# Token attention: the score products of one batch mixed with the query and key projections of a batch two periods younger

## The reference

```python
def _L1_attn_b_ref(x, Wq, Wk, Wv, Wo, bo, lq1, lq2, lk1, lk2):
    q = _split_qk(x @ Wq.T, b, n) * SCALE      # (b, n, 32 half-heads, 8)
    k = _split_qk(x @ Wk.T, b, n)
    v = (x @ Wv.T).reshape(b, n, H, 2 * D).transpose(0, 2, 1, 3)
    att = jax.nn.softmax(jnp.nan_to_num(jnp.einsum('bnqd,bnkd->bnqk', q, k)), axis=-1)
    diff = att[:, :, :H, :H] - lam * att[:, :, H:, H:]
    out = jnp.einsum('bnah,bhnd->bnad', diff, v)
    out = out * rsqrt(mean(out * out, -1) + EPS) * (1.0 - LAM_INIT)
    return out.reshape(b, n, DIM) @ Wo.T + bo
```

## Time and profile before

| | |
|---|---|
| median of three runs | 1204.39 us (1202.14 to 1208.55) |
| the profiled execution: its span | 1204.3 us |
| busy in it: PE, DVE, ACT, GpSimd | 1006.6, 714.8, 367.6, 319.5 us |
| span of B1's scores, first of batch 0 to last of batch 7 | 799.5 to 1034.8 us |

### The profile page before, as it was taken

The page is one execution under the profiler, slowest core; times in us unless marked ns, Lnnn a source line. Parts: engine busy times, 40 slices in busy tenths (PEclk is TensorE's granted clock), DMA queues, the critical chain, the costliest instruction groups (busy, mean ns, idle before and its releaser), DMA issues.

```text
span 1204.3 us, 21333 instructions
## 1 busy us (share of the span) xinstructions
PE 1006.6 (84%) x8146; PEld 883.3 (73%) x8146; DVE 714.8 (59%) x1323; ACT 367.6 (31%) x663; POOL 319.5 (27%) x352
## 2 busy tenths in 40 slices
PE   3589988665779787788879999998888887799998
PEld 3466755445667665656658999998888887799998
DVE  4458775534667777876664554545566654644443
ACT  2136554422322222242333322321222221232222
POOL 4102220027754573221110031100333332330000
PEclk9569998886889989987768999976677775599999
DMA  8735340000120002554410000335666665210000
GB/s 231 213 117 169 125 117 24 2 1 18 28 79 1 1 1 65 172 175 124 134 33 1 2 1 1 74 78 105 122 132 131 132 132 88 36 36 10 19 18 19
DMA packets 147429, 89.38 MB, mean 74 GB/s; under 512 B 109632, under 2 KB 136256, under 8 KB 146560
## 3 DMA queue, kind: packets, MB, share of 16 engines
q1 hardware_dynamic: 142960, 70.45, 24.0%
q10 hardware_dynamic: 2944, 12.59, 3.6%
q0 software_dynamic: 1424, 4.98, 1.4%
HBM read 54.16 MB, written 33.55 MB: 73 GB/s over the span
## 4 chain that ended last, share of the span: by engine, by line
PE 63%; DVE 19%; issue 6%; ACT 4%; SPq 3%; DMA 2%; POOL 2%; DVEq 0%; ACTq 0%; POOLq 0%
PE SC L373 16%; PE SC L2145 9%; PE pb L373 8%; PE OT L373 7%; PE pa L373 4%; PE OT L1893 3%; DVE mx L1319 3%; PE SC L1846 2%; PE SC L1875 2%; PE OT L2172 2%; PE OT L2070 2%; PE pa L2340 2%; DMA b_Q<-q_groups 1%; DVE OS L1487 1%; DVE ON L1676 1%
## 5 line engine op out<-in xcount | busy, mean ns | idle before, releaser
L373 PE MATMUL SC<-xT_h,w_h 128*128 128x256 f32 x512 | 148.6, 290 | 10.0 <-DVE xT_l L1736 7.8
L373 PE MATMUL SC<-xT_l,w_h 128*128 128x256 f32 x512 | 146.9, 287 | 0.0
L373 PE MATMUL SC<-xT_h,w_l 128*128 128x256 f32 x512 | 146.1, 285 | 0.0
L373 PEld LDWEIGHTS SC<-xT_h,w_h 128*128 128x128 f32 x512 | 98.9, 193 | 13.4 <-DVE xT_l L1736 11.5
L1319 DVE TENSOR_REDUCE mx<-SC 128x4 f32<-128x1024 f32 x64 | 78.1, 1221 | 48.3 <-PE SC L1846 47.9
L373 PE MATMUL OT<-w,Qs 128*128 128x256 f32 x768 | 104.3, 285 | 2.2 <-DVE Qs L1746 1.4
L373 PEld LDWEIGHTS SC<-xT_h,w_l 128*128 128x128 f32 x512 | 99.1, 194 | 0.0
L373 PEld LDWEIGHTS SC<-xT_l,w_h 128*128 128x128 f32 x512 | 98.6, 193 | 0.0
L373 PEld LDWEIGHTS OT<-w,Qs 128*128 128x128 f32 x768 | 96.4, 191 | 2.8 <-DVE Qs L1746 1.6
L1742 DVE TENSOR_TENSOR hidden_f<-SC,silu_gate 128x512 f32<-128x512 f32 x64 | 44.1, 689 | 76.7 <-ACT silu_gate L1199 76.7
L1746 DVE TENSOR_TENSOR Qs<-hidden_f,Qs 128x512 fp32r<-128x512 f32 x64 | 44.7, 698 | 44.7 <-ACT Qs L1207 44.7
(11 more groups left out here) (413 smaller groups left out, 2693.7 us busy)
## 6 DMA issues: line engine op xcount, KB each, us to landing
Qs<-q_stack SPq DMA_DIRECT2D x56, 128.0 KB, 2.9
k_stack<-KT_h SPq DMA_DIRECT2D x16, 256.0 KB, 2.4
k_stack<-KT_l SPq DMA_DIRECT2D x16, 256.0 KB, 3.0
q_stack<-QT_h SPq DMA_DIRECT2D x16, 256.0 KB, 2.2
q_stack<-QT_l SPq DMA_DIRECT2D x16, 256.0 KB, 2.8
b_Q<-q_groups SPq DMA_DIRECT2D x64, 64.0 KB
o_groups<-b_O ACTq DMA_DIRECT2D x8, 512.0 KB, 2.9
Qs<-q_stack SPq DMA_DIRECT2D x56, 64.0 KB, 3.1
```

What stands on the lines that cost most here:

```text
L373: ins = pe.matmul(out_ap, left[a], right[b], start=first and n == 0, stop=last and n == len(terms) - 1, **more)
```

## The change

The work on each batch stays the same; its place changes. `q_out` and `k_out` no longer issue their products: they only hold their waits. The new `mixed(g, h)` issues the 32 score products of half h of batch b and, between them, the 12 projection products of batch b+2: those of the queries in half 0, those of the keys in half 1. One projection product follows each second or third score product, and the twelfth follows the last. What leads up to the projections and what follows them is moved to fit:

- x_turned(b+3), and the high and low parts of x, come one slot earlier, in slot 7, and so before y_out and turned of the next period
- the parts of Q are made in slot 0 (two slots earlier), those of K in slot 1 (two slots earlier)
- stats, rstd and xn come one slot earlier (3, 4 and 6).

v_out, the stores and the loads keep their slots. In DVE's `at_slot` the line of less_maximum(b, 0) stands ahead of that of K's low part, and both are due in slot 1; weights_of(b, 0) is due in slot 2. On ACT, load_k and load_q of batch b+1 stand ahead of K's high part in slot 1.

```diff
--- before.py
+++ after.py
@@ -809,7 +809,7 @@
                             prepare([A0_JOBS[g]])
 
                 def tokens_at(g):
-                    for b in due(g, -19):
+                    for b in due(g, -20):
                         rstd_of(b)
                     for b in due(g, 11):
                         clipped(b)
@@ -1140,13 +1140,13 @@
                         load_k(b)
                     for b in due(g, -7):
                         load_q(b)
-                    for b in due(g, -16):
+                    for b in due(g, -17):
                         high(b, x_pair(s, b), pa, "xT", "vp", 1, "xh")
                     for b in due(g, 18):
                         high(b, aT, OT[1], "aT", "y", 1, "ah")
-                    for b in due(g, -14):
+                    for b in due(g, -16):
                         high(b, QT, pb, "qp", "qstore", 64, "qh")
-                    for b in due(g, -13):
+                    for b in due(g, -15):
                         high(b, KT, pa, "kp", "kstore", 64, "kh")
                     for b in due(g, 3):
                         probs(b, 1)
@@ -1607,17 +1607,17 @@
                         less_maximum(b, 1)
                     for b in due(g, 18):
                         low(b, aT, OT[1], "ah", "al")
-                    for b in due(g, -14):
+                    for b in due(g, -16):
                         low(b, QT, pb, "qh", "ql")
                     for b in due(g, 13):
                         square_sums(b)
-                    for b in due(g, -13):
+                    for b in due(g, -15):
                         low(b, KT, pa, "kh", "kl")
                     for b in due(g, 4):
                         weights_of(b, 1)
-                    for b in due(g, -20):
+                    for b in due(g, -21):
                         stats(b)
-                    for b in due(g, -17):
+                    for b in due(g, -18):
                         normalise(b)
                 return at_slot
 
@@ -2122,11 +2122,19 @@
                     wait("xres", b - 5, 1)
                     if b == 0:
                         split_done(pe, "attn_b1")
-                    channels_out(pb, wq, "qp", x_pair(s, b))
 
                 def k_out(b):
                     wait("xl", b, 1)
-                    channels_out(pa, wk, "kp", x_pair(s, b))
+
+                def projected(b, ps, w, signal, n):
+
+                    of = x_pair(s, b)
+                    o, t, term = n // 6, n % 6 // 3, n % 3
+                    i, j = ((0, 0), (0, 1), (1, 0))[term]
+                    ins = pe.matmul(ps[:, o * S:(o + 1) * S], w[i][:, t, o * P:(o + 1) * P], of[j][:, t, :],
+                                    start=t == 0 and term == 0, stop=t == 1 and term == 2)
+                    if n == 11:
+                        ins.then_inc(sig.sem[signal], 1)
 
                 def v_out(b):
                     wait("ql", b, 1)
@@ -2139,11 +2147,28 @@
                     wait("clamped", b - 1, h + 1)
                     if b == 0:
                         item(pe, F5, "g_hid", B - 1, 3 + h)
+
+                def scored(b, h, n):
+
                     Kg = b1_K[b % 2].rearrange("p (k g) -> p k g", g=GROUPS)
+                    g = HALVES * h + n
+                    ins = pe.matmul(SC[h][:, 32 * n:32 * n + 32], b1_rows(Qg, g), b1_rows(Kg, g), start=True, stop=True)
+                    if n == HALVES - 1:
+                        ins.then_inc(sig.sem["scores"], 1)
+
+                def mixed(g, h):
+
+                    front, back = due(g, h - 16), due(g, h)
+                    for b in front:
+                        (q_out, k_out)[h](b)
+                    for b in back:
+                        scores(b, h)
                     for n in range(HALVES):
-                        g = HALVES * h + n
-                        ins = pe.matmul(SC[h][:, 32 * n:32 * n + 32], b1_rows(Qg, g), b1_rows(Kg, g), start=True, stop=True)
-                    ins.then_inc(sig.sem["scores"], 1)
+                        for b in back:
+                            scored(b, h, n)
+                        for b in front:
+                            if n * 12 // HALVES < (n + 1) * 12 // HALVES:
+                                projected(b, (pb, pa)[h], (wq, wk)[h], ("qp", "kp")[h], n * 12 // HALVES)
 
                 def b1_rows(q, g):
                     return q[0:96, :, g]
@@ -2191,20 +2216,15 @@
                     for h in range(TT):
                         for b in due(g, 8):
                             turned(b, h)
-                    for b in due(g, -16):
+                    for b in due(g, -17):
                         x_turned(b)
                     for h in range(TT):
                         for b in due(g, 9):
                             attend(b, h)
                     for h in range(TT):
-                        for b in due(g, h):
-                            scores(b, h)
+                        mixed(g, h)
                     for b in due(g, 18):
                         a_turned(b)
-                    for b in due(g, -14):
-                        q_out(b)
-                    for b in due(g, -13):
-                        k_out(b)
                     for b in due(g, -12):
                         v_out(b)
                 return at_slot
```

## The result

The changed kernel takes 1280.9 us (median of 4, 1276.0 to 1287.6), the kernel before 1203.3 us (median of 4). The ratio is 1.0655, with a 95% interval of 1.0616 to 1.0695: slower by 78 us. The forecast was 1281. Some executions of a kernel fall in a slower state of the chip, and the ratios here, and the medians of kernels 2 and 8, are of the others alone, so that they can differ by a tenth of a per cent from the quotient of two medians.

What follows compares the result with a forecast made beforehand. PE was taken as fullest but not quite full, its 13.8 us gap ending in a wait for DVE's xn. Stall and dearer halves summed to +56 us (full clock) or +83.9 (half); +77 taken on 1204 gave 1281, range 1248 to 1308.

Steps and rivals of the forecast that it cites:

- The stall on DVE: K's low part waits past the second half's scores, pushing weights_of(b, 0) and later work back: steady gap +11.3 us at half clock.
- T: The end of the second half's score products of batch b, from which the gap to the next batch is counted.
- ACT's load issues: K's high part on ACT stands behind load_q's four DMA issues, which add 2.9 us to DVE's wait.
- y_out and turned: PE work at the gap's end, after x_turned: 2.72 and 3.51 us at half clock.
- The halves: 32 score products with 12 wide ones between: 9.28 us at half clock or 8.39 at full, against 6.94 for narrow alone.
- Rival 2: Switching does not overlap: each wide product costs load plus stream, 0.40 us; about 1300 us and up; 7 in 100.
- wide products wholly hidden: Lower bound of a mixed half: wide products vanish under narrow loads, leaving 6.94 us.
- rival 1: Same stall, cheap halves: clock stays full or wide products hide beneath narrow loads; 1260 down to 1243 us; 14 in 100.
- Three quarters of the way to half clock: Clock assumed between the sums at full clock (+56 us) and half clock (+83.9): +77 us.
- mixing by itself is near nothing: Two halves cost +4.8 us per period against 3.76 leaving the gap; net within -3.8 to +6.
- the landing at +13: The b_Q loads land about 13 us after the second half's scores, taken as hidden in the longer gap.
- Rival 3: Wide products vanish under narrow loads and DVE is not late: six gaps lose 3.76 us each, 1182 us; 4 in 100.

Runs made afterwards that it cites:

- Kernel 2: The changed kernel with only ACT's K high part moved ahead of load_q, behind load_k: 1263.0 us, 1.0507 of before.
- kernel 8: The kernel before, unmixed, with the younger batch's norm made earlier from batch 3 on: 1199.2 us, 0.9961 of before.
- Kernel 1: The changed kernel with only DVE's K low part moved from slot 1 to slot 2: 1238.2 us, 1.030 of before.
- kernel 7: The kernel before with one more wait: DVE begins weights_of(b, 0) only after both halves of batch b's scores: 1223.0 us, 1.0158 of before.
- kernel 4: The changed kernel with both moves, K low in slot 2 on DVE and K high ahead of load_q on ACT: 1234.0 us, 1.0274 of before.
- kernel 5: kernel 4 with the younger batch's statistics, root, xn and x_turned made earlier from batch 3 on: 1224.9 us, 1.0205 of before.
- kernel 10: kernel 5 with the b_Q loads split six on SP and six on ACT: 1226.8 us, 1.021 of before.
- kernel 9: kernel 8 with the b_Q loads split six on SP and six on ACT: 1199.2 us, 0.9978 of before.
- Kernel 6: kernel 5 unmixed, each half's 32 score products first and its 12 projection products behind them: 1218.2 us, 1.0142 of before.
- kernel 3: The changed kernel, same slots, unmixed: each half's 32 score products first, then its 12 projection products: 1270.8 us, 1.0572 of before.

## Why the prediction was right

**The stall on DVE** was right in place and size. Expected after T: KT_l done at 4.2, weights_of(b, 0) 7.55, less_maximum 11.3, weights_of(b, 1) 16.4, xn 17.85, x_turned 18.9. Read: 4.2, 7.6, 11.3, 16.1, 17.5, 18.6. Kernel 1 shows the cause, by an edit on DVE alone that takes 43 us away; kernel 7 shows a part of it, by a wait that brings some 20 us into the kernel before.

**ACT's load issues** as a part of the stall: right. Kernel 2 gives 18 us for a wait that is 2.4 to 2.6 us shorter in six periods, where 17 was expected (12.5 us of it stand in the gaps of its trace), and kernel 4 shows that the issues cost only in the stall's shadow.

**y_out and turned** were priced at half clock throughout, 6.2 us, and then a quarter of the way back: they took 2.56 and 1.9, that is 4.5, behind batch 3. The granted clock was 0.50 in y_out, 0.85 in the first microsecond of turned and 1.00 in the second. The gap was 23.1, where the sum at half clock had 25.1. Batches 0, 1 and 5 measured 21.4, 21.4 and 19.1 against 21.1, 21.7 and 19.3.

**The halves** were expected at 9.28 us at half clock and 8.39 at full. They took 8.8 to 9.2, and 0.2 for the last wide product. The mixed stretch can be read in the chain of batch 3, at both clocks:

```profile
932.17 0.22 PE pb L2134
932.39 0.55 PE SC L2155 x3
...
938.11 0.40 PE pb L2134
938.50 0.45 PE SC L2155 x3
```

One wide and three narrow products take 0.77 us at full clock and 0.85 at half. Three narrow alone are 0.65, so a wide one adds 0.12 or 0.20: the 0.121 and 0.195 of the forecast, which came from a wide run's pace and from one switch. By the Trainium skill ("TensorE: Matmul & The Clock Gate", section LDWEIGHTS) a load of 128 columns takes an estimated 107 ns, and a wide product would have added that at half clock. The trace does not agree: it has 0.20. Rival 2 (0.40 each) and wide products wholly hidden are both excluded, and so is the cheap end of rival 1.

**The match to a microsecond is luck.** Three quarters of the way to half clock was a choice between +56 and +83.9. The trace has 75.2, which is 69% of the way, and the four executions lie 12 us apart. Batches 2 to 4 lost 14.2, 13.7 and 13.7 us, where the sum has 16.1 at half clock and 10.65 at full. Two small things stood at nothing: batch 6 gained 1.6 us, and the first score product came 1.4 us later.

**What was wrong** is a sentence that did not enter the sum: that mixing by itself is near nothing, since 3.76 us leave the gap. They do not come off the gap. Once the stall is taken away (kernels 5 and 10), the gaps of batches 0 to 5 are 12.2 to 14.6 us, where they were 13.3 to 14.2 before. The chains behind batch 4 end in the wait for b_Q, which is there 13.1 to 13.9 us after its first issue, whoever issues it, and the wide products had lain beside that transfer. The prediction had read the landing at +13 and called it hidden, but did not set it against the 3.76. So the mixed halves cost their full 2.1 us each, 12 halves or 25 us, and kernel 5 is 24 us behind the kernel before. Rival 3 with its 1182 us was out of reach for the same reason: in the steady batches the transfer holds the gap at about 13 us.

The loss by its parts, from the differences of the ratios (6.55, 3.00, 2.74 and 2.05%, of 1203 us): 43 us by the keys' low part ahead of weights_of(b, 0), 3 more with ACT's order (within the noise of the two runs), 8 by the norm and x_turned in the tail (kernel 4 to 5), and 25 by projections moved from beside the b_Q transfer into the halves. Each difference is uncertain by several microseconds. The last part is borne out by kernels 9 and 10: they differ by the projections' place and the queue moves that go with it, and 24.5 us of the difference of their traces lie in the halves. Kernel 6, which has the same places and does not mix, is still 17 us behind the kernel before, but by another chain (QT_l and load_out), so that the place and the mixing are not cleanly told apart. That the gap does not shrink because of b_Q is read from the chains; no kernel has a faster transfer.

Open is why y_out and turned get half clock behind some batches and full clock behind others, which makes kernel 7's gap 19.3 us behind two batches and 15.5 to 17.2 behind the others, and where the few microseconds of kernel 8 come from, since its trace was not usable.

## What to carry to other kernels

When a product is moved, move the place of what drains it only after reading who stands behind the drain in each queue: here one line of DVE's order, one slot too early, turned 3.3 us of hidden work into a gap 5 to 7 us longer in each of six periods. Work that fills a gap is free as long as something else (here a transfer) sets the gap's length, and costs its full time where it is put instead; ask first what the gap would be without it. And mixing wide and narrow products does not make the wide ones free: here a wide one in the mix costs 0.12 us at full clock and 0.20 at half, about what it does in a row of its own (0.121 and 0.213).

## What the runs showed of the hardware

- Behind batch 4 the 12 b_Q loads (64 KB each) are all there 13.1 to 13.9 us after the first is issued, with eight on SP and four on ACT (13.2, kernel 5) or six and six (13.1 and 13.9, kernels 9 and 10). A last issue that came sooner only had a longer way to the landing (8.2, 9.2, 10.0 us). It is no fixed time: behind batch 1 of kernel 9 the next score product started 11.3 us after the first issue.
- DVE's multiplication of 64 partitions by 512 twice took 2.40 to 2.41 us where GpSimd's addition of 128 x 512 ran beside it for 1.15 us, and 1.38 to 1.39 in each of the 73 cases in which no GpSimd instruction ran beside it, in the traces of both kernels and of kernels 1 to 3. A move that shortens a wait can so bring two instructions together.
- The narrow products seem to keep their pace in the mix too: three take 0.65 us in a row of their own at either clock, and a mixed group rises from 0.77 us at full clock to 0.85 at half, by 0.08 us, where a wide product alone would rise by 0.09.
